# Side tasks in pairs on every second step, output projection one step later, loads grouped by first use, head and tail reordered: a macaron block (half FFN, attention, half FFN)

## The reference

```python
def ffn(h):                              # h: layernormed tokens
    query = h @ Wq.T                     # 64 wide
    rq, rk = query @ Wr.T, aux_keys @ Wr.T
    router = rq @ rk.T / sqrt(48) + log_rel
    top_idx = top_k(router, 8)
    attn = query . aux_keys[top_idx] / sqrt(64) + log_rel[top_idx]
    aux = softmax(attn) . aux_values[top_idx]
    aux = aux @ Wvd.T @ Wvu.T
    log_var = log1p(var(h))
    u = clip(0.5 * log_var / mean(log_var) + 2.5 * sigmoid(gelu(h @ Wu1.T + bu1) @ Wu2.T + bu2), 0, 5)
    gate = sigmoid(gate_w1 * clip((u - 0.5) / 1.5, 0, 1) + gate_bias)   # 0 below 0.05
    return h + gate * aux

def attn(h):
    q, k, v = rope(h @ Wq), rope(h @ Wk), h @ Wv      # 32, 8, 8 heads of 128
    p = softmax(causal(q @ k.T / sqrt(128)))
    return (p @ v) @ Wo + bo

x = x + 0.5 * ffn(layernorm(x))
x = x + attn(layernorm(x))
x = x + 0.5 * ffn(layernorm(x))
```

## Time and profile before

| what | us |
|---|---|
| median of 3 runs | 1541.02 |
| lowest and highest of them | 1540.57, 1544.21 |
| the profiled execution's own time | 1551.33 |
| span of the profiled execution | 1549.5 |
| PE busy in it | 1420.2 (92%) |
| DVE busy | 1222.1 (79%) |
| ACT busy | 882.3 (57%) |
| POOL busy | 527.7 (34%) |

### The profile page before, as it was taken

One profiled execution on the slowest core, in us unless ns is written; L12 is line 12 of the kernel. 1 busy time (PEld: TensorE's weight loads), 2 busy tenths in 40 slices (PEclk: granted clock), 3 DMA queues, 4 the chain that ended last, 5 costly groups with the idle time before them and its releaser, 6 DMA issues.

```text
span 1549.5 us, 26280 instructions
## 1 busy us (share of the span) xinstructions
PE 1420.2 (92%) x8962; PEld 800.1 (52%) x8962; DVE 1222.1 (79%) x3119; ACT 882.3 (57%) x2170; POOL 527.7 (34%) x441
## 2 busy tenths in 40 slices
PE   3487998999999999999899999999899999999966
PEld 2244554455555555555555555555455555555533
DVE  2767878998888788877888887888788888778745
ACT  1346675667666565555556655565555666555524
POOL 0255555555542322323333322223333233223202
PEclk9788999999999999999999999999999999999988
DMA  6127666776755554544455554654455565544522
GB/s 220 41 67 183 178 156 166 187 188 163 168 140 144 126 118 99 129 115 112 116 139 129 124 106 112 136 107 110 113 139 134 135 133 134 125 113 120 105 52 109
DMA packets 409539, 201.12 MB, mean 130 GB/s; under 512 B 352160, under 2 KB 353376, under 8 KB 409408
## 3 DMA queue, kind: packets, MB, share of 16 engines
q1 hardware_dynamic: 407296, 195.25, 52.6%
q10 hardware_dynamic: 2112, 4.19, 0.8%
HBM read 90.30 MB, written 25.17 MB: 75 GB/s over the span
## 4 chain that ended last, share of the span: by engine, by line
PE 70%; DVE 13%; ACT 6%; issue 4%; POOL 3%; SPq 2%; DMA 2%; POOLq 0%; ACTq 0%; DVEq 0%
PE PJ L1047 16%; PE PJ L1049 16%; PE PJ L1048 16%; PE PV L1047 4%; PE PV L1049 4%; PE PV L1048 4%; PE SC L1202 3%; PE SC L1203 3%; PE SC L1204 3%; ACT p L565 3%; DVE phl L874 2%; POOL t L436 2%; DVE p L863 2%; DMA pTf<-phl 1%; DVE t L836 1%
## 5 line engine op out<-in xcount | busy, mean ns | idle before, releaser
L436 POOL TENSOR_TENSOR t<-t 128x512 f32<-128x512 f32 x160 | 202.9, 1268 | 744.5 <-DVE t L836 744.3
L565 ACT ACTIVATE p<-p,mn 128x512 f32<-128x512 f32 (+3 forms) x512 | 281.7, 553 | 191.2 <-DVE mn L863 191.0
L874 DVE SCALAR_TENSOR_TENSOR phl<-p,ri,phl 128x512 f16<-128x512 f32 (+3 forms) x512 | 292.7, 595 | 0.0
L574 ACT ACTIVATE phl<-p,ri 128x512 f16<-128x512 f32 (+3 forms) x512 | 245.1, 552 | 14.8 <-DVE ri L959 12.0
L1047 PE MATMUL PJ<-XTh,wsp 128*128 128x512 f16 x640 | 244.3, 382 | 1.4 <-DVE XTl L718 1.4
L1048 PE MATMUL PJ<-XTl,wsp 128*128 128x512 f16 x640 | 244.1, 381 | 0.0
L1049 PE MATMUL PJ<-XTh,wsp 128*128 128x512 f16 x640 | 244.1, 381 | 0.0
L1047 PE MATMUL PJ<-wosp,oTf 128*128 128x512 bf16 x512 | 197.4, 386 | 29.8 <-issue 24.4
L863 DVE CUSTOM_DVE_ANT_0 p<-SC,maskw 128x512 f32<-128x512 f32 (+3 forms) x512 | 220.0, 485 | 4.9 <-PE SC L1204 3.1
L1049 PE MATMUL PJ<-wosp,oTl 128*128 128x512 bf16 x512 | 197.7, 386 | 0.0
L1048 PE MATMUL PJ<-wosp,oTf 128*128 128x512 f16 x512 | 197.3, 385 | 0.0
(11 more groups left out here) (178 smaller groups left out, 2595.2 us busy)
## 6 DMA issues: line engine op xcount, KB each, us to landing
wsp<-kept SPq DMA_DIRECT2D x144, 256.0 KB, 2.9
wosp<-kept SPq DMA_DIRECT2D x96, 256.0 KB, 3.1
raw<-in_wqkv SPq DMA_DIRECT2D x48, 256.0 KB, 3.7
kept<-wsp SPq DMA_DIRECT2D x48, 256.0 KB, 2.3
raw<-in_wo SPq DMA_DIRECT2D x32, 256.0 KB, 4.3
pTf<-phl SPq DMA_TRANSPOSE x512, 2.9
kept<-wosp SPq DMA_DIRECT2D x32, 256.0 KB, 2.9
X<-in_x ACTq DMA_DIRECT2D x4, 1024.0 KB, 10.7
```

The lines of the kernel that those rows point to most:

```text
L436: nc.gpsimd.tensor_tensor(t1[:, j, :], t1[:, j, :], t2[:, j, :], ALU.add).then_inc(rope_sum, 1)
L565: ins = nc.scalar.activation(pt, pt, ACT.Exp, bias=mn[:, par, i:i + 1], scale=-1.0, accum_out=rs[:, par, i:i + 1])
L574: nc.scalar.activation(phl[:, par, POFF[i]:POFF[i] + w], p[:, par, SOFF[i]:SOFF[i] + w], ACT.Copy, scale=ri[:, par, i:i + 1]).then_inc(a_p ...
L874: nc.vector.scalar_tensor_tensor(out=phl[:, par, POFF[i] + w:POFF[i] + 2 * w], in0=p[:, par, SOFF[i]:SOFF[i] + w], scalar=ri[:, par, i:i + 1],
```

## The change

1. The tables of side tasks are rewritten. Two tiles of a stage now share a step, and PE's side tasks stand on even steps only. Stages of HID, HOUT, min, exp and others move to other steps, top comes a step after its scr on DVE.
2. In a step, DVE, ACT and POOL now do the side tasks before `rest_of` (K, V, O); PE had this order already. `normal_of` alternates between `hb` and the `asc` tile, so that two normalized tiles can stand at once.
3. The output projections move one step later: O(n-1, 0) comes at h = 2. `LAST` therefore holds six of them. Behind `attend(NS - 2)` PE first does the two of the unit before, then heads 0 to 2 of the last unit's four, and only their head 3 after `attend(NS - 1)`. The weight table `REFILL` moves W0 to W3 accordingly.
4. The 14 small loads get five semaphores by first use, in a new order (`fwrT`, `fkeyT`, `fwr`, `fwq` first). The loads of weights and rope tables wait for the third load of x.
5. Head: the setup uses four PSUM banks in place of two; the layernorm transposes of batch 0 go before the products of the value weights; moments of later tiles are spread between other DVE work; the mask penalty goes before the weight splits on POOL; the six weight splits of ACT are spread behind the softmax and gate steps; Q0 goes before V; `add_bias` of batch 0 goes behind the first ropes.
6. Tail: HID before SCR; the gate is computed once for all 16 tiles instead of for 12 and then 4; ET goes behind 6 AUX tiles instead of 8; tile 15 is added by DVE; the last store is two of 512 KB.

```diff
-PE_A = {2: [("LT", 0, 0)], 3: [("LT", 0, 1)], 4: [("LT", 0, 2)], 6: [("LT", 0, 3)], 7: [("SCR", 0, 0)],
-        8: [("HID", 0, 0)], 10: [("SCR", 0, 1)], 11: [("HOUT", 0, 0)], 14: [("ET", 0, 0)],
+PE_A = {2: [("LT", 0, 0), ("LT", 0, 1)], 4: [("LT", 0, 2), ("LT", 0, 3)], 6: [("SCR", 0, 0)], 8: [("SCR", 0, 1)],
+        10: [("HID", 0, 0)], 12: [("HOUT", 0, 0), ("ET", 0, 0)], 18: [("AUX", 0, 0), ("AUX", 0, 1)],
+        20: [("AUX", 0, 2), ("AUX", 0, 3)], 24: [("LT", 1, 0), ("LT", 1, 1)], 26: [("LT", 1, 2), ("LT", 1, 3)]}
+PE_B = {12: [("LT", 2, 0), ("LT", 2, 1)], 14: [("LT", 2, 2), ("LT", 2, 3)], 16: [("SCR", 1, 0)], 22: [("SCR", 1, 1)],
+        28: [("HID", 1, 0)], 30: [("ET", 1, 0), ("HOUT", 1, 0)]}
...
-    r = {0: [("O", n - 2, 3, 0)], 1: [("K", n + 1, 0, 0), ("O", n - 1, 0, 0)], 2: [("O", n - 1, 1, 0)],
-         3: [("V", n + 1, 0, 0), ("O", n - 1, 2, 0)]}[h]
+    r = {0: [("O", n - 2, 2, 0)], 1: [("K", n + 1, 0, 0), ("O", n - 2, 3, 0)], 2: [("O", n - 1, 0, 0)],
+         3: [("V", n + 1, 0, 0), ("O", n - 1, 1, 0)]}[h]
...
+LAST = [("O", NU - 2, 2, 0), ("O", NU - 2, 3, 0)] + [("O", NU - 1, i, 0) for i in range(4)]
...
+HEAD = ([("LT", 0, 0, i) for i in range(4)] + [("SCR", 0, 0, 0), ("SCR", 0, 0, 1), ("HID", 0, 0, 0), ("HOUT", 0, 0, 0),
+        ("MEAN", 0, 0, 0), ("ET", 0, 0, 0)] + [("AUX", 0, 0, i) for i in range(4)] + [("LT", 1, 0, i) for i in range(4)])
+FIRST = [("K", 0, 0, 0), ("Q", 0, 0, 0), ("V", 0, 0, 0), ("Q", 0, 1, 0)]
...
+TAIL = ([("LT", 2, 3, i) for i in range(4)] + [("HID", 1, 3, 0), ("MEAN", 1, 0, 0), ("SCR", 1, 3, 0), ("SCR", 1, 3, 1),
+        ("HOUT", 1, 3, 0)] + [("AUX", 1, 0, i) for i in range(4)] + [("AUX", 1, 1, 0), ("AUX", 1, 1, 1), ("ET", 1, 3, 0),
+        ("AUX", 1, 1, 2), ("AUX", 1, 1, 3)] + [("AUX", 1, b, i) for b in range(2, 4) for i in range(4)])
...
+REFILL = {0: [(1, "Q1"), (1, "V"), (-1, "W3")], 1: [(1, "Q2")], 2: [(1, "Q3"), (2, "K"), (0, "W0")],
+          3: [(2, "Q0"), (0, "W1"), (0, "W2")]}
...
+            sp.wait_ge(ld_x[2], 16)
+            for r in range(4):
+                raw_load(r)
...
-            pe.wait_ge(ld_f, 16 * NFL)
-            mm(PV[0:RDIM, 0:NSLOT], fwrT[:, :], fkeyT[:, :], start=True, stop=True).then_inc(fs_pe, 1)
+            pe.wait_ge(ld_fr, 48)
+            mm(PJ[0:RDIM, 3, 0:NSLOT], fwrT[:, :], fkeyT[:, :], start=True, stop=True).then_inc(fs_pe, 1)
...
+        def setup_bank(c):
+            return (SC[:, c, :] if c < 3 else PV[:, :])[:, 0:2 * NSLOT]
...
+            penalty(0, 0)
             for r in range(6):
                 weight_low(r)
-            penalty(0, 0)
-            for i in range(4):
-                add_bias(0, i)
             for kind, n, idx, _ in FIRST:
                 if kind in "QK":
                     rope(kind, n, idx)
             weight_low(6)
+            for i in range(4):
+                add_bias(0, i)
...
             attend(NS - 2)
-            for kind, n, idx, _ in LAST[:1]:
+            for kind, n, idx, _ in LAST[:2]:
                 project(kind, n, idx)
+            pe.wait_ge(o_lo, NS - 1)
+            for h in range(HG):
+                piece_ready(NU - 1, f"W{h}")
+            for task in LAST[2:]:
+                free(task)
+                project_out(NU - 1, task[2], range(HG - 1))
             attend(NS - 1)
-            for kind, n, idx, _ in LAST[1:]:
-                project(kind, n, idx)
+            pe.wait_ge(o_lo, NS)
+            for task in LAST[2:]:
+                project_out(NU - 1, task[2], range(HG - 1, HG)).then_inc(s_o, 1)
```

More of the change, by code:

```diff
@@ L26 @@
 NROPE = 4
-NFL = 14
 SOFF = [896, 1024, 512, 0]
@@ L74, in side @@
+ACT_B = {7: [("root", 2, 0)], 12: [("hi", 2, 0), ("hi", 2, 1)], 13: [("xup", 2, 0), ("xup", 2, 1)],
+         14: [("hi", 2, 2), ("hi", 2, 3)], 15: [("xup", 2, 2), ("xup", 2, 3)], 25: [("exp", 1, 0)],
+         28: [("gelu", 1, 0)], 30: [("et", 1, 0)]}
+POOL_A = {9: [("pen", 0, 0)], 26: [("bob", 1, 0), ("bob", 1, 1)], 27: [("bob", 1, 2), ("bob", 1, 3)]}
+POOL_B = {23: [("pen", 1, 0)]}
 def side(table_a, table_b, s):
@@ L260, in rope_index, with evens @@
             return 5 * n if kind == "K" else 5 * n + idx + 1
+        odd = [1, 3, 5, 7, 9, 11, 13]
         def odd_tile(f, n):
-            return f == 1 and n % 2 == 1
+            return f == 1 and n in odd
+        def evens(n):
+            return n - len([m for m in odd if m < n])
         def consumed(task):
@@ L460, in _ @@
                         add_bias(bb, i)
+                for kind, m, _, _ in rest_of(n, h):
+                    if kind == "K":
+                        rope("K", m, 0)
                 for it in refills(s):
@@ L469, in _ @@
             penalty(1, B - 1)
-            for n in range(1, NT, 2):
+            for n in odd:
                 aux_add(n)
@@ L633, in _ @@
                         gate_exp(2 * bb + i, 4 * bb, 4 * bb + 4)
+                for kind, m, _, _ in rest_of(n, h):
+                    if kind == "K":
+                        rope("K", m, 0)
+                    if kind == "V":
+                        value_hi(m)
                 for it in refills(s):
@@ L1002, in _ @@
                         moments(1, 4 * bb + i)
+                for kind, m, idx, _ in rest_of(n, h):
+                    if kind == "K":
+                        rope(kind, m, idx)
+                    if kind == "V":
+                        value_lo(m)
+                    if kind == "O":
+                        project_add(m, idx)
             for k in range(TB):
@@ L1134, in halves, with project_out @@
                 return w[:, 0, :].bitcast(BF16), w[:, 1, :]
+            def project_out(n, idx, heads):
+                ts = lo_slice(idx)
+                for h in heads:
+                    wh, wl = halves(f"W{h}", n)
+                    ins = mm3(bank(("O", n, idx, 0)), oTh[:, n % 2, h, ts], oTl[:, n % 2, h, ts], wh, wl,
+                              h == 0, h == HG - 1)
+                return ins
             def project(kind, n, idx):
```

323 lines of the change are left out of this document (166 added, 157 removed).

## The result

| kernel | median, us | lowest and highest | profiled execution, own time | its span |
|---|---|---|---|---|
| before | 1541.65 (4 runs) | 1540.57, 1544.21 | 1551.33 | 1549.5 |
| after | 1502.55 (4 runs) | 1500.57, 1506.38 | 1500.57 | 1498.3 |

The change makes the kernel faster: the ratio of the times is 0.9747, with a 95% interval of 0.9724 to 0.977, that is 39 us less. I had forecast 1475, with a range of 1450 to 1512. The range held, the middle was 27.5 us too low.

A forecast was written before the change was run, and what follows sets the result against it. PE was taken to bound the loop, and chains across engines the head and tail. Gains of 26 + 18 + 18 + 4 = 66 us from 1551.3 gave 1485.3 profiled, less 10.3 a median of 1475 us, range 1450 to 1512.

The forecast's parts named there:

- The head: Stretch up to the first scores: earlier first matmul, gated sum and Q0 save 26 us, bounds 20 and 32.
- Batches 1 to 3: Loop after batch 0: O waits 18.1 and clock 6 gained, less 6 for a new wait, gives 18 us.
- The one new wait I saw: Step 12, batches 1 and 2: O waits 2.5 us for the first LT's bank; 6 us together with the clock.
- my 6 us: Batches 1 to 3: granted clock no longer falling after O's waits, taken as 6 us together.
- the 3.5 of slack: Odd loop steps: `attend` has some 3.5 us of slack to absorb DVE's lateness from paired even steps.
- Batch 0: First loop batch: O waits 10.0 plus 8.7 of probability waits, less 1, gives 18 us; bounds 5 and 35.
- half of the probability waits (8.7): Batch 0: half of PE's 17.3 us of waits for transposed probabilities goes, 8.7 us.
- rival B: Loop: the waits only move, so head and tail alone count, 1541 - 30 = 1511 us; chance 0.22.
- The tail: After the loop: earlier moments and shorter ET wait against a later gate, net gain 4 us, bounds -3 and 10.
- The offset: Whole kernel: 10.3 us subtracted because the profiled execution of before lay that far above its median.
- A: Whole kernel: the forecast itself, 1475 us, its own range 1460 to 1495; chance 0.55.
- D: Loop: DVE late in paired even steps, `attend` waits, costing 108 us against 56 won elsewhere, 1593 us; chance 0.06.

The follow-up runs named there:

- the second profile: The kernel after run once more, without an edit, on another chip: 1502.01 us, head 75.8 us.
- e3_o_only: The kernel before with only the output projection one step later; old tables, step order, head and tail: 1533.69 us.
- e5_step13: The kernel after with HOUT, ET and the gates behind them moved from step 12 to step 13: 1498.61 us.
- e6_no_split: The kernel after with POOL's subtraction for the weights' low halves replaced by a fill with zeros: 1489.37 us.
- e2_loop_only: The kernel before with the new loop (tables, side-task order, O a step later); old head and tail order: 1519.02 us.
- e9_bias_first: The kernel after with POOL's four bias additions put back ahead of the first ropes: 1503.77 us.
- e1_before: The kernel before run once more, without an edit, for a second profile: its profiled execution took 1547.7 us.

## Why the prediction was right or wrong

**The head: right.** Forecast -26, measured -27.0 (-23.8 in the second profile). First matmul at 9.4 us (forecast 8.5), root at 17.05 (16), first gated sum at 46.75 (47), first scores at 72.6 (73). Two terms behind the sum were off against each other: from the sum to the first K matmul 14.2 us (12.3), from there to the scores 11.6 (13.8). (68.85 less 47 is 21.9 and not the 21.6 of my sum, which changes nothing.) The rows of the kernel after:

```profile
9.39 0.66 PE L1261 MATMUL PJ<-fkeyT,fwrT 64*48 64x128 f32 x2 [9.39 <-DMA fwr<-in_f_wr]
...
17.05 0.20 ACT L499 ACTIVATE sd<-ve 128x4 f32<-128x4 f32 x1
...
46.75 0.75 DVE L856 SCALAR_TENSOR_TENSOR X<-PJ,gs,X 128x512 f32<-128x512 f32 x1
...
60.98 0.38 PE L1095 MATMUL PJ<-XTh,wsp 128*128 128x512 f16 x1 [1.45 <-DVE XTl L751]
...
72.59 0.38 PE L1255 MATMUL SC<-kTl,qTh 128*128 128x512 f16 x1 [1.00 <-POOL qTl L456]
```

**Batches 1 to 3: right.** Forecast -18, measured -19.5. O's waits of 18.1 us are gone, and e3_o_only shows that this alone would not have done it. The one new wait I saw, 2.5 us in step 12 of two batches, is there with 2.78 and 2.95 us, at the bank named; e5_step13 shows that with what hangs on it it costs 8.8 us, not the 6 I charged (bounds 0 and 12). That the total fits is in part luck: without this wait (e5_step13) the three batches gain 28.3 us, where my terms gave 24. The granted clock of batch 2, for which I took part of my 6 us, stayed at 0.99 in the kernel after, and 3.6 us of probability waits went for which I had no term. Two readings ahead of the sum were off as well. The steps of the earlier trace rows that I called h = 1 and h = 2 are steps 123 and 124, h = 3 and h = 0; steps with h = 1 and 2 take the same 11.0 and 8.4. And by my own terms a paired step leaves DVE 2.2 to 3.2 us late, not 2 to 2.7, which is still inside the 3.5 of slack.

**Batch 0: wrong, by 11 us.** The step that failed is "half of the probability waits (8.7)" together with the O waits of 10.0. The waits of O went, but those for probabilities grew from 17.3 to 22.2, with 3.8 on the score bank; the sum of all waits stayed (31.1 and 30.1). What was gained, 6.8 us, is the O that now lies behind the loop (2.6), 1.0 of waits, and a rest of 3.2. The granted clock rose from 0.96 to 0.98 there, which has the right sign, but its two digits can't settle 3 us, and no run takes it apart. So rival B, which I gave 0.22 for the whole loop, holds in batch 0 alone, and what I had given as the lower bound, 5 us "if DVE's lateness only moves from O to `attend`", is what happened. I had the reason in hand: I wrote that the change takes nothing of the slowing away, and still took half of the waits as gone. The slowing did stay: the low halves take 761 ns in the mean before and 777 after in batch 0. e6_no_split shows what the splitting is worth: 11 us of batch 0, the waits down to 14.7. I should have asked what makes the DVE late there, not how the other waits would follow.

**The first steps behind the shorter head.** I charged 1 us for `add_bias`. e2_loop_only does steps 0 to 5 in 59.6 us and the full change in 64.4; e9_bias_first gets 2.8 of these 4.8 back and loses 3.3 behind them. Work that the head no longer holds stands in the first steps, on a DVE that is without a pause from 81 to 99 us.

**The tail: wrong, by 6 us.** Forecast -4 (bounds -3 and +10 of gain), measured +2.1, close to its lower bound. Some of this is only where the cut lies: the sixth O, 2.6 us of matmuls, moved from the loop into the tail, and I had called it "moved, not added" without charging either stretch. Without it the tail is 0.5 shorter. Two terms failed behind that. The first is the part up to the last moments, which I had 2.5 us earlier: they end 0.9 later, or 1.7 earlier without the sixth O, because PE fills the last wait but now waits 3.00 us ahead of the `attend` before it. The second is the gate. I put its delay at some 5 us; the scales come 12.4 us later than with the old order (60.0 and 47.5 behind the last scores), and ET starts later although it waits less. POOL's last sums didn't shrink from three to two (three are 3.85 us in the earlier trace rows) but grew to four in a row, 5.26 us, which I put down to AUX tiles bunched behind the late gate; no run shows that apart.

**The offset: wrong, by 12 us, and no part of the kernel.** I took 10.3 us from the sum since before's profiled execution lay that far above the median. The kernel after lies 2.0 below its median in the same comparison. In spans the forecast was 66 and the measurement 51.2; in medians 66 and 39.1. So 15 us of the 27.5 were the sum's fault and 12 the profiled execution of before. What was longer in that execution stays open: e1_before, 3.7 us shorter in span, has 3.0 of these in its loop, spread over three batches.

Of the rivals, A was right in the three later batches and the head, B in batch 0, D (slower) nowhere: no `attend` wait in batches 1 to 3 is longer than 1.1 us. The paired even steps fit, with the slack I had worked out from the steps' lengths. The 56 us that D has "won elsewhere" follow from none of my terms, whose sum is 66.

## What to carry to other kernels

Moving a waiting instruction later on its engine gains only as much as the next waiter has slack: O's move alone gave 8 us for the 28 us of waits that I had counted, and 20 once the side work was placed so that the DVE was in time. So before counting a wait as removed, work out for the stretch in question what makes the late engine late; where that cause stays (here: two-input DVE instructions beside a POOL that reads SBUF), count nothing. And when a few banks go round in turn, look which task takes the bank of which: a side task moved by one step, out of the step with the most bank users, was worth 4 us a batch.
